# A one-core transformer block: one GpSimd step moved and eight filler matmuls placed in the tail

## The reference, cut to what matters

```python
x_diff = x[:, None, :, :] - select_mean_diff[None, :, None, :]
x_diff = x_diff / jnp.linalg.norm(x_diff, axis=3, keepdims=True)
cont = jnp.einsum('nds,bntd->bnts', select_weight, x_diff) ** 2
score = cont.sum(axis=-1)
gate = jax.nn.sigmoid(imp_slope[None, :, None] * (score - imp_center[None, :, None]))
sel_scale = gate.max(axis=1)[..., None]
...
mod_x = jnp.einsum('btdh,btd->bth', upd, x_debias)
degen_up = jnp.einsum('btdh,bth->btd', dgn, mod_x)
mod_x_bias = ETA * (bias + degen_up)
return (1.0 - sel_scale) * x + sel_scale * mod_x_bias
...
h = h + _L0_attn_ref(_layernorm(h, axis=-1), ...)
h = h + _L0_ffn_ref(_layernorm(h, axis=-1), ...)
```

## Time and profile before

| | |
|---|---|
| median of three runs | 841.18 us |
| the profiled execution's own time | 840.35 us |
| its span in the trace | 838.6 us |
| TensorE busy | 746.5 us (89%) |
| VectorE busy | 587.1 us (70%) |
| ScalarE busy | 453.9 us (54%) |
| GpSimd busy | 436.3 us (52%) |
| mean granted TensorE clock | 0.974 |

### The profile page before, as it was taken

One profiled execution on the slowest core, in us unless ns is written; L12 is line 12 of the kernel. 1 busy time (PEld: TensorE's weight loads), 2 busy tenths in 40 slices (PEclk: granted clock), 3 DMA queues, 4 the chain that ended last, 5 costly groups with the idle time before them and its releaser, 6 DMA issues.

```text
span 838.6 us, 19677 instructions
## 1 busy us (share of the span) xinstructions
PE 746.5 (89%) x6944; PEld 682.8 (81%) x6944; DVE 587.1 (70%) x1631; ACT 453.9 (54%) x1246; POOL 436.3 (52%) x657
## 2 busy tenths in 40 slices
PE   0066778899999999999999999999999999999985
PEld 0055757799999999999999999999999998899762
DVE  7979957777775665666666656666655777777877
ACT  6633316555555656555565565555756644554420
POOL 0076934555554746444447464444747566556522
PEclk9998988899999999999999999999999999999996
DMA  9013460100010102000001020000100000000002
GB/s 207 0 41 63 84 242 25 39 2 0 0 33 6 51 2 76 0 0 0 0 1 51 1 77 0 0 0 0 37 16 2 1 2 26 25 25 25 1 25 75
DMA packets 30533, 26.46 MB, mean 32 GB/s; under 512 B 22476, under 2 KB 22860, under 8 KB 30228
## 3 DMA queue, kind: packets, MB, share of 16 engines
q1 hardware_dynamic: 30196, 25.71, 10.7%
q10 hardware_dynamic: 288, 0.13, 0.1%
HBM read 17.44 MB, written 8.39 MB: 31 GB/s over the span
## 4 chain that ended last, share of the span: by engine, by line
PE 78%; DVE 13%; issue 3%; POOL 3%; ACT 2%; DVEq 0%; DMA 0%; SPq 0%; ACTq 0%
PE bank L1199 17%; PE bank L1201 17%; PE bank L1200 17%; PE bank_pair L1201 4%; PE bank_pair L1199 4%; PE bank_pair L1200 4%; POOL w_lo L421 2%; DVE bank_pair L887 2%; PE bank L1339 2%; PE bank_pair L1339 2%; PE bank_pair L1349 1%; PE bank L1353 1%; PE bank L1349 1%; PE bank L1292 1%; PE bank L1211 1%
## 5 line engine op out<-in xcount | busy, mean ns | idle before, releaser
L1199 PE MATMUL bank<-xt_hi,w_hi 128*128 (+1 forms) x768 | 216.6, 282 | 1.6 <-POOL w_lo L421 0.8
L1201 PE MATMUL bank<-xt_lo,w_hi 128*128 (+1 forms) x768 | 214.4, 279 | 0.0
L1200 PE MATMUL bank<-xt_hi,w_lo 128*128 (+1 forms) x768 | 214.3, 279 | 0.0
L968 DVE TENSOR_TENSOR kq<-bank,cst 128x512 f32<-128x512 f32 (+1 forms) x96 | 57.9, 603 | 140.2 <-ACT swap L655 106.6
L466 POOL TENSOR_TENSOR swap<-swap,cst 128x512 f32<-128x512 f32 (+1 forms) x96 | 105.7, 1103 | 81.5 <-ACT swap L655 80.0
L1199 PEld LDWEIGHTS bank<-xt_hi,w_hi 128*128 128x128 f32 x768 | 144.3, 188 | 3.0 <-issue 1.6
L1201 PEld LDWEIGHTS bank<-xt_lo,w_hi 128*128 128x128 f32 x768 | 144.2, 188 | 0.0
L1200 PEld LDWEIGHTS bank<-xt_hi,w_lo 128*128 128x128 f32 x768 | 144.1, 188 | 0.0
L349 POOL TENSOR_TENSOR spare<-cst 1x1 f32<-1x1 f32 x87 | 16.6, 191 | 226.4 <-DVE rinv L1102 141.2
L695 ACT ACTIVATE sm<-sm,mx 128x128 f32<-128x128 f32 (+1 forms) x256 | 113.6, 445 | 21.7 <-DVE mx L1092 21.6
L654 ACT ACTIVATE swap<-bank 64x512 f32<-64x512 f32 (+1 forms) x96 | 50.3, 523 | 124.9 <-PE bank L1201 122.1
(11 more groups left out here) (251 smaller groups left out, 1922.7 us busy)
## 6 DMA issues: line engine op xcount, KB each, us to landing
mixed<-st SPq DMA_DIRECT2D x32, 128.0 KB, 2.0
out<-x SPq DMA_DIRECT2D x16, 256.0 KB, 2.1
raw<-in_w_qkv SPq DMA_DIRECT2D x8, 384.0 KB, 3.5
raw<-in_w_o SPq DMA_DIRECT2D x10, 256.0 KB, 2.5
x<-mixed SPq DMA_DIRECT2D x2, 1280.0 KB, 10.2
norm_mem<-in_w_qkv SPq DMA_DIRECT2D x6, 384.0 KB, 3.7
x<-mixed SPq DMA_DIRECT2D x3, 512.0 KB, 4.7
norm_mem<-in_w_o SPq DMA_DIRECT2D x6, 256.0 KB, 2.9
```

The lines of the kernel that those rows point to most:

```text
L968: v.tensor_tensor(view(kq), src, table(cosT), ALU.mult).then_inc(kq_cos, 1)
L1199: mmul(dst, lh, rh, start=start and k == 0, stop=False, skip_group_check=True)
L1200: mmul(dst, ll, rh, start=False, stop=False, skip_group_check=True)
L1201: last = mmul(dst, lh, rl, start=False, stop=stop and k == n - 1, skip_group_check=True)
```

## The change

On GpSimd `add_normed(5)` moves ahead of the norm of batch 7. On TensorE eight filler matmuls come in: one after the update of batch 5, one after the transposes of batch 7, three after the gate product of batch 7, and three after the update of batch 6. `keep_warm` gets a second argument for the bank (0 for the first two, 3 for the others). Two waits move: the wait for the reads of the gate products (now for the 7th read, ahead of the first filler), and the wait for the last attention output's addition (now ahead of the first three fillers on bank 3, whose content that addition reads).

```diff
--- before.py
+++ after.py
@@ -519,8 +519,8 @@
 
             normalise_probs(NG * NB - 1)
             norm(2 * NB - 2)
+            add_normed(NB - 3)
             norm(2 * NB - 1)
-            add_normed(NB - 3)
             add_normed(NB - 2)
 
 
@@ -1240,10 +1240,10 @@
                 last = mmul(banks[7][:, 0:FC], ones[:], pw[:, k, 0:FC], start=k == 0, stop=k == KC - 1)
             last.then_inc(cw_mm, 1)
 
-            def keep_warm(count):
+            def keep_warm(count, bank=0):
 
                 for _ in range(count):
-                    mmul(banks[0][:], ident, cst[:, 0:512], start=True, stop=True)
+                    mmul(banks[bank][:], ident, cst[:, 0:512], start=True, stop=True)
 
             pe.wait_ge(evac, NQ)
             keep_warm(5)
@@ -1443,16 +1443,19 @@
             gate_product(NB - 2)
             update_rows(NB - 3)
             update_product(NB - 3)
+            pe.wait_ge(f_read, NB - 1)
+            keep_warm(1)
             pe.wait_ge(xn_ready, 2 * NB)
-            pe.wait_ge(f_read, NB - 2)
             transpose_tokens(2 * NB - 1, 1)
-            pe.wait_ge(f_read, NB - 1)
+            keep_warm(1)
             pe.wait_ge(xt_hi, 2 * 2 * NB)
             gate_product(NB - 1)
+            pe.wait_ge(x_added, 2 * last + 2)
+            keep_warm(3, 3)
             update_rows(NB - 2)
             update_product(NB - 2, 1)
+            keep_warm(3, 3)
             update_rows(NB - 1)
-            pe.wait_ge(x_added, 2 * last + 2)
             update_product(NB - 1, 3)
```

## The result

The changed kernel has a median of 836.20 us over six runs (835.22 to 837.82). The kernel before, timed beside it, has 841.13 us over six (838.55 to 843.98). The ratio is 0.9948, with a 95% interval of 0.9924 to 0.9972.

A forecast was written before the change was run, and what follows sets the result against it. TensorE bounds most of the kernel, but VectorE's chain bounds the tail, lengthened by GpSimd and TensorE's clock. −2.67 + 0.46 − 0.43 = −2.64 us from 841.18 gives 838.5 us, 0.3% faster; range 837.2 to 841.0.

The forecast's parts named there:

- The moved add: GpSimd's add of batch 5, placed earlier, gives VectorE back 0.39 us in batch 7's normalisation and 2.28 in batch 6's steps.
- the small step comes free when GpSimd does: VectorE's L1038 of batch 7 ends at 826.81 us, as GpSimd's add of batch 6 ends at 826.77.
- That pair only moves earlier, as one: Batch 7's small steps and GpSimd's add of batch 6 keep their trouble; both just start earlier, no further gain.
- Batch 7's chain cannot pass L1038 before GpSimd's add ends: On VectorE, batch 7's L1038 is held until 824.56 us, so even a slow gate product would be hidden.
- The first filler: It holds TensorE until 816.57 us, delaying the transposes, their ScalarE copies and batch 6's exponential: 0.46 us cost.
- The triples and the last tile: Three fillers twice on TensorE keep full clock, so VectorE's last tile no longer waits: 0.43 us gained.
- The output transfers follow VectorE's adds as before: At the kernel's end, transfers were taken to keep their distance behind VectorE's last adds; no term in the sum.
- Sum of the tail: Terms −2.67 + 0.46 − 0.43 give −2.64 us; the forecast's own range is −1.9 to −3.2 us.
- The level: Whole kernel's time: median 841.18 − 2.64 = 838.5 us, range 837.2 to 841.0 including the scatter of the median.
- The moved add's own cost: Slowdown of VectorE's L1005 beside the moved GpSimd add: taken as nothing, bounds 0 and 0.4 us.
- The clock rival: TensorE's clock falls all the same near 818.4 us: 838.9 us, or 843.5 if it falls again; chance 0.09.
- It doesn't do what it says.: VectorE's long steps have another cause than GpSimd's instructions, so no change, 841.2 us; chance 0.05.

The follow-up runs named there:

- pad on VectorE: Changed kernel with two more unused statistics instructions (0.65 us each) on VectorE ahead of batch 7's gate read; ratio to the kernel before 0.9973.
- the pad on GpSimd: Changed kernel with one more unused scaling (0.68 us) on GpSimd between batch 5's add and the norm of batch 7; ratio to the kernel before 0.9958.
- the two repeats: The kernel before and the changed kernel, each profiled again without alteration; tails 27.13 and 24.35 us, ratios to the kernel before 1.0003 and 0.9958.
- the repeat: The changed kernel run once more, unaltered, against the kernel before; ratio 0.9958 (0.9943 to 0.9974).
- the repeat of before: The kernel before run again unchanged, as a null and for a second profile; ratio 1.0003 (0.9983 to 1.0022).

## Why the prediction was wrong, point by point

- **The moved add.** Right: 2.67 us were forecast for L950 and batch 6's steps, and the move alone took 7.56 − 4.88 = 2.68 us off that stretch, with the norm of batch 7 not delayed.
- **The cause of the long steps.** The forecast had "the small step comes free when GpSimd does", without saying which steps. The runs narrow it: a step with two SBUF inputs waits for the end of the one GpSimd add beside it (L1035 at 1.22 us beside an add, at 0.15 without), and L1036 and L1039, with one input, stay short beside the same adds. By the Trainium skill (SBUF — State Buffer, "Summary: rules for kernel authors") the second of the two to issue waits in full until the first is done, where VectorE has two SBUF inputs and GpSimd reads SBUF. The trace agrees for GpSimd's adds. It doesn't for its scaling in the changed kernel: L1035 started at 819.12 with 0.15 us, within the scaling that runs from 818.36 to 819.75, while L1037 beside it ended with it (819.50 + 0.26 = 819.76). Nor does this cover 0.38 us of the gain, the normalisation: L950 reads one tensor from SBUF, and before it took 1.38 us beside GpSimd's scaling, which itself took 1.86 us instead of 1.36 (and the rows above). The two held each other up there; by what is not shown.
- **Batch 7's chain.** "That pair only moves earlier, as one" failed: 0.39 us came on top. "Batch 7's chain cannot pass L1038 before GpSimd's add ends" failed too. In the changed kernel L1038 is done at 821.02, while GpSimd adds until 822.20. GpSimd's scaling of batch 6 now starts 818.36 − 817.95 = 0.41 us after batch 6's L1062, and not 0.32 as before (822.95 − 822.63), though it is free long before. The steps meet its instructions otherwise: L1035 is not caught, and L1039 gets in ahead of its end. In the profiles, all five kernels with the moved add, the old add of batch 6 and no pad on VectorE have 0.41 to 0.42 us and a chain of 6.80 or 6.81 us, and all three with the add in its old place 0.32 us and 7.20 to 7.22. The gate read is not the cause: with the pad on GpSimd it comes 0.23 us after L1062, almost as before, and the chain takes 6.81. GpSimd's spare instruction ahead of the scaling starts 0.04 to 0.05 us behind L1062 in all eight, so the 0.09 us lie between it and the scaling, on GpSimd itself; why they are there stays open. That they are what saves the 0.39 us is argued from the rows, since no run moved this start alone. The pad on VectorE shows the other side: a gate read that came 1.1 us later than in the changed kernel was not hidden.
- **The first filler.** 0.46 us forecast, 0.29 measured (0.64 − 0.35, and 5.17 − 4.88). The mechanism is right. The size was off because I let the exponential wait for the end of the copies' 1.09 us: it starts 815.88 − 814.91 = 0.97 us after they begin.
- **The triples and the last tile.** 0.43 us forecast, 0.52 measured on VectorE (6.09 − 5.57), and 0.39 of it lost behind it. "The output transfers follow VectorE's adds as before" failed, and the sum has no term for it: SyncE's last issue comes 0.56 us behind VectorE's end instead of 0.20, since its loop needs 1.50 us for two tiles and VectorE 1.32.
- **Sum of the tail.** −2.64 forecast, −2.90 measured (27.21 to 24.31), and −2.78 between the two repeats. The tail was forecast to 0.3 us, partly by luck: batch 7's chain gave 0.39 us that was not forecast, and SyncE's lag took 0.39. What is left is the filler (0.17) and the last tile (0.09). In the forecast's own range the lower end, with a free exponential, is −2.64 − 0.46 = −3.1 and not −3.2.
- **The level.** This is the step that put the median out of the range. It was formed as 841.18 − 2.64, and below the forecast's own lower end (841.18 − 3.2 = 838.0) the range of 837.2 to 841.0 left only 0.8 us for "the scatter of the median". That term was too small: the last L1005 of one and the same program lies at 809.09 and at 812.05, and over 35 runs the kernel before spans 838.10 to 843.71 us. The median of six runs of the changed kernel is 836.20 us and that of twelve others 837.26, so the same program moved by 1.06 us, and the second median lies just inside the range. The ratio's interval of 2.4 to 6.4 us, and 2.2 to 4.8 us in the repeat, both hold 2.9. That some gain ahead of the tail is real is not excluded by the totals, but no profile shows one.
- **The moved add's own cost.** Right at nothing, but read from rows that did not show it: the L1005 at 710.2 and 784.2 lie beside GpSimd's scalings (783.66 to 785.01), not beside its adds. The L1005 of the changed kernel lies beside an add, at 0.69 us.
- **The clock rival.** It did not come about: the clock held through TensorE's work in the tail of all profiles with fillers, but for the last product of the fillers alone. Whether the transposes count for the clock no run here tells. The move alone and the repeat of before show that the gate product can have full clock without them; 12 of all 13 profiles have it. The chance of 0.09 could not have changed the time much: with the clock down the gate product cost nothing before, and with the move alone the half-clock last product costs 0.37 us on VectorE, which come back because SyncE's issues then do not lag.
- **"It doesn't do what it says."** It holds for the fillers: with them the tail is 0.24 us longer than with the move alone. Their total is a cost or nothing.

## What to carry to other kernels

Where small dependent VectorE steps set the end, look for GpSimd instructions that read SBUF beside them; moving one batch's to a place where VectorE reads PSUM or takes statistics took 2.7 us off the path here. Taking batch 6's away from the chain as well took 1.9 us more (6.81 to 4.87). Fillers for TensorE's clock paid here only where a product was the last to arrive: count how far the next engine is behind it, clock down, before placing any, and look whose queue they hold up. Where the last results come close together, look at the issuing engine's own loop too: its issues, and not the transfers, fell behind here. Where start-up scatters by 2 us and more, judge a change in the tail from a landmark to the end, and give a median of few runs its scatter in the range.

## What the runs showed that I had not expected

- With GpSimd's instructions 0.09 us later beside the same steps of VectorE, these took 6.81 us instead of 7.20.
- TensorE's clock fell at batch 7's gate product in one of two profiles of the kernel before (3.76 and 2.09 us for the same 16 passes), with the same work ahead of it.
- SyncE's loop of two 256 KB transfers a turn takes 1.50 us a turn, 0.89 us of it across the turn's end. With VectorE's adds 0.66 us apart the last issue lags by 0.56 us and the span ends 3.05 to 3.13 us behind VectorE; where VectorE paused ahead of its last add, it is 0.20 us and 2.60 to 2.68 us.
- The first projection starts between 118.5 and 122.8 us in kernels whose programs up to there are the same, which is the larger part of the spread of the last L1005.
